# Attention plan: maxima placed by a count of VectorE's work against TensorE's

## The reference

```python
attn = jnp.einsum('bhqd,bhkd->bhqk', q, k) / np.sqrt(HD)
attn = jnp.where(mask[None, None], -jnp.inf, attn)
attn = jax.nn.softmax(attn, axis=-1)
out = jnp.einsum('bhqk,bhkd->bhqd', attn, v)
```

## Time and profile before

| | us |
|---|---|
| median of 3 runs | 1292.87 |
| lowest and highest | 1291.17, 1295.96 |
| the profiled execution | 1295.78 |
| its span, first to last instruction | 1294.5 |
| PE busy in it | 1202.9 |
| DVE busy | 897.0 |
| ACT busy | 661.0 |
| POOL busy | 602.1 |

### The profile page before, as it was taken

How to read it: one execution, slowest core, us unless ns; L and a number is a source line. 1 busy time by engine, 2 the same in 40 slices (tenths; PEclk the granted TensorE clock), 3 DMA queues, 4 the chain that set the end, 5 groups by cost and what they waited for, 6 DMA issues and landing times.

```text
span 1294.5 us, 22123 instructions
## 1 busy us (share of the span) xinstructions
PE 1202.9 (93%) x7422; PEld 781.6 (60%) x7429; DVE 897.0 (69%) x2100; ACT 661.0 (51%) x1313; POOL 602.1 (47%) x496
## 2 busy tenths in 40 slices
PE   4899999989998999999999999989999989999996
PEld 3578888758776554444545455545444447777774
DVE  7767777679996666575667677587754685666664
ACT  2545555525546554354456566356567733444442
POOL 5835445314200111001426556465682373888886
PEclk9899999999999999999989999999999999999999
DMA  9923333565620032023345845656743353666665
GB/s 345 354 90 109 105 114 107 163 181 104 109 48 32 4 68 34 1 96 50 86 124 139 164 99 111 183 131 157 138 99 66 109 210 74 104 103 101 101 103 73
DMA packets 68557, 148.52 MB, mean 115 GB/s; under 512 B 8832, under 2 KB 29312, under 8 KB 64448
## 3 DMA queue, kind: packets, MB, share of 16 engines
q0 software_dynamic: 35184, 93.34, 34.2%
q1 hardware_dynamic: 33264, 53.77, 12.1%
HBM read 81.28 MB, written 33.55 MB: 89 GB/s over the span
## 4 chain that ended last, share of the span: by engine, by line
PE 60%; DVE 17%; DMA 9%; issue 7%; POOL 4%; ACT 3%; SPq 0%; DVEq 0%; POOLq 0%; ACTq 0%
PE bank L1637 10%; PE bank L839 9%; PE bank L1649 9%; PE bank L997 8%; PE bank L862 5%; PE bank L1667 4%; PE bank L1704 3%; DMA out<-Y,DI 3%; DMA XG<-xn,TK 3%; POOL out L789 3%; DVE PM L1010 3%; DVE bank L1012 2%; PE bank L821 2%; PE bank L1398 2%; DMA CD<-P 1%
## 5 line engine op out<-in xcount | busy, mean ns | idle before, releaser
L1756 ACT ACTIVATE P<-bank 128x512 f32<-128x512 f32 (+3 forms) x640 | 303.8, 535 | 259.4 <-PE bank L1637 252.7
L1010 DVE TENSOR_REDUCE PM<-bank 128x1 f32<-128x512 f32 x384 | 252.8, 686 | 82.5 <-PE bank L997 81.9
L1637 PE MATMUL bank<-Qs,Ks 98*128 98x512 f32 (+3 forms) x640 | 241.1, 407 | 5.0 <-ACT P L1756 2.8
L997 PE MATMUL bank<-Ks,Qs 96*128 96x512 f32 (+3 forms) x640 | 234.6, 387 | 10.7 <-DVE PM L1012 5.4
L1637 PEld LDWEIGHTS bank<-Qs,Ks 98*128 98x128 f32 x640 | 116.9, 190 | 130.8 <-issue 59.5
L1795 POOL TENSOR_SCALAR_AFFINE_SELECT P<-P 128x512 f32<-128x512 f32 x64 | 42.9, 682 | 284.6 <-ACT P L1756 234.9
L1012 DVE CUSTOM_DVE_ANT_0 bank<-bank,KB 128x128 f32<-128x128 f32 (+3 forms) x256 | 124.8, 499 | 56.5 <-PE bank L997 55.9
L997 PEld LDWEIGHTS bank<-Ks,Qs 96*128 96x128 f32 x640 | 121.5, 191 | 57.6 <-DVE PM L1010 17.3
L1649 PE MATMUL bank<-P,V 128*32 128x512 f32 (+3 forms) x1280 | 150.9, 543 | 3.9 <-POOL P L1795 3.9
L789 POOL DMA_INDIRECT out<-Y,DI x78 | 127.1, 1629 | 40.7 <-issue 33.9
L1809 POOL TENSOR_TENSOR CH<-CH,P 128x512 f32<-128x512 f32 x108 | 139.3, 1438 | 14.0 <-ACT P L1756 13.3
(11 more groups left out here) (190 smaller groups left out, 1987.8 us busy)
## 6 DMA issues: line engine op xcount, KB each, us to landing
CD<-P POOLq DMA_DIRECT2D x17, 1024.0 KB, 7.3
xn<-XN SPq DMA_DIRECT2D x8, 1024.0 KB, 7.1
WR<-L_ffn_w POOLq DMA_DIRECT2D x16, 512.0 KB, 15.4
XO<-y POOLq DMA_DIRECT2D x8, 1024.0 KB, 9.8
WR<-L_ffn_w SPq DMA_DIRECT2D x16, 512.0 KB, 8.4
CD<-P SPq DMA_DIRECT2D x7, 1024.0 KB, 5.2
CD<-CH POOLq DMA_DIRECT2D x7, 1024.0 KB, 7.0
XA<-y POOLq DMA_DIRECT2D x24, 256.0 KB, 4.2
```

Source lines behind the costliest of these rows:

```text
L997: pe.matmul(bk(g, bank)[:, 0:n], g.Qs[b][0:96, G % 4 * 4 + h, c * P:c * P + P], g.Ks[0:96, G % 4, k * BQ:k * BQ + n], start=True, stop=Tru ...
L1010: dve.tensor_reduce(dst, bk(g, bank)[:, 0:n], AX.X, ALU.max).then_inc(s(f"free{bank}"), 1)
L1637: pe.matmul(bk(g, bank)[:, o:BQ], g.Ks[0:98, G % 4, k * P:k * P + P], g.Qs[G // 4][0:98, G % 4 * 4 + j, o:BQ], start=True, stop=True).then ...
L1756: act.activation(a.P4[buffer_of(n)][:, j, o:BQ], bk(g, score_bank(g, i))[:, o:BQ], ACT.Exp, scale=scale).then_inc(s("exp"), 1)
```

## The change

The widths are replaced by a count of work. A new class `Load` adds up, over the plan so far, units of PE's work (a full-width score or top is 1, a weigh 5 or 9, others from a table) and of DVE's work (a full-width top is 2.9, others from a table). Behind each score the count is brought up to date once, and then in up to two rounds a top is added unless DVE's count is above 0.81 of PE's. The start of the scores with five banks now looks for the last top or foundcopy and goes 2 steps behind it, where it looked for the last top and went 8 steps behind.

```diff
+DVE_SHARE = 0.81
+
+class Load:
+
+    PE = {"proj": 15, "tsum": 3, "even": 4, "found": 3, "turn": 2, "logits": 5, "best": 1}
+    DVE = {"proj": 3, "stats": 3, "solve": 6, "scale": 2.5, "tsum": 1, "even": 3, "solvemax": 3, "logits": 1.5, "best": 4.5}
+
+    def __init__(self):
+        self.pe = self.dve = 0.0
+
+    def add(self, plan, counted):
+        for step in plan[counted:]:
+            kind = step[0]
+            if kind in ("score", "weigh"):
+                G, k = TILES[step[1]]
+                wide = (BQ - first(G // 4, k)) / BQ
+                self.pe += wide if kind == "score" else wide * (8 if step[1] in SUMMED else 4) + 1
+            elif kind == "top":
+                wide = 1 if step[4] < step[1] // 4 else (step[3] + 1) / 4
+                self.pe += wide
+                self.dve += 0.6 + 2.3 * wide
+            else:
+                self.pe += self.PE.get(kind, 0)
+                self.dve += self.DVE.get(kind, 0)
+        return len(plan)
...
-    told, weight, given, extra, known, copying, free = 4, 0.0, 0.0, [], [], [], True
+    told, extra, known, copying, free, load, counted = 4, [], [], [], True, Load(), 0
...
             plan.append(("score", n, j))
-            weight += (BQ - first(b, k)) / BQ
-            while ahead and given < 1.1 * weight:
+            counted = load.add(plan, counted)
+            for _ in range(2):
+                if not ahead or load.dve > DVE_SHARE * load.pe:
+                    break
                 key = ahead.pop(0)
-                given += 1 if key[4] < key[1] // 4 else (key[3] + 1) / 4
                 plan.append(key)
...
-    last = max(at for at, step in enumerate(plan) if step[0] == "top")
-    g.wide = min(4 * step[1] + step[2] for step in plan[last + 8:] if step[0] == "score")
+    last = max(at for at, step in enumerate(plan) if step[0] in ("top", "foundcopy"))
+    g.wide = min(4 * step[1] + step[2] for step in plan[last + 2:] if step[0] == "score")
```

## The result

| | us |
|---|---|
| changed kernel, median of 4 runs | 1322.72 (1320.48 to 1326.5) |
| kernel before, same comparison | 1294.29 (1291.17 to 1295.96) |
| ratio, 95% interval | 1.0215 (1.0193 to 1.0237) |
| span of the profiled execution | 1322.2 |

The change makes the kernel 2.2% slower, 28 us. I had forecast slower, by 10 us, with a range up to 1318. The direction and the main term, waits for a bank behind bursts of tops, were right; what the change gives back was mis-sized, and score waits that I had put at nothing were not nothing.

A forecast was written before the change was run, and what follows sets the result against it. PE sets the pace, with DVE costing it some 22 us. Terms 18 + 3 + 1.5 - 3 - 3.5 - 4.5 - 1.5 = +10 us give 1305.8, on the median's scale 1303 us; range 1285 to 1318.

The forecast's parts named there:

- (1): Tops in bursts wait for their PSUM bank: 24.6 us after, less 6.6 now, +18 us.
- (2): Runs of six and eight tops are held by DVE's 0.60 us a top: +3 us.
- The 1.18 us: Full-width tops: a bank's next user starts 1.18 us, or five units, after the top that held it.
- Rival A, relief wins: PE's waits at tile ends are the dear ones, nearly all 22 us come back: 1283 us, chance 0.15.
- (3): Tops behind found wait longer for the bank that ScalarE's copy at L1068 frees: +1.5 us.
- (4): PE's waits for DVE backlog go: found -3 us, tsum and L1667 -3.5, tops -4.5.
- The 4.5 us for backlog: Tops' waits behind projections, statistics and best shrink as the count slows tops there: -4.5 of 5.9 us.
- (5): At 599 to 603 us found and best no longer share a tile: -1.5 us, with its clock.
- (6): The end: last top and five-bank scores start later, no DMA or Pool step moves but maxima copies: 0.
- My signs: L997 weight loads wait 40 us or more in over 100 places, L1059 under 4 us; wrong if PEclk drops.
- rival C: PE's short gaps make its clock drop, ten more drops at 1.6 us: 1319 us, chance 0.1.

The follow-up runs named there:

- e1: Kernel before with its old budget, but two tops whenever one is due: 1304.8 us, 1.0078.
- e2: Changed kernel, same table and 0.81, but counted after each top and the coming weigh counted in quarters: 1304.62 us, 1.0068.
- e11: Kernel before with tops in pairs and DVE reading half of each top's columns: 1275.37 us, 0.9845.
- e3: Changed kernel with DVE reading only half of each top's columns (half maxima): 1296.6 us, 1.0016.
- e6: Kernel before with only the change's last two lines, the later start of five-bank scores: 1296.5 us, 1.0002.
- e9: Changed kernel with half maxima, variance by tensor_reduce and a copy in place of ScalarE's square root in the statistics: 1286.6 us, 0.9937.
- e10: Kernel before with half maxima, variance by tensor_reduce and a copy in place of ScalarE's square root in the statistics: 1267.44 us, 0.9797.
- e5: Changed kernel with the statistics' variance made by tensor_reduce instead of L299's tensor_scalar, 1e-5 left out: 1321.01 us, 1.0195.

## Why the prediction was wrong, point by point

*Bank waits and long runs, (1) and (2): right.* Forecast +18 and +3, measured +21.7 where a top follows a top. The subtraction in (1) was not clean: it took 6.6 us, reckoned without the correction for earlier waits, from 24.6, reckoned with it. Like for like it is 24.6 - 4.2 = +20.4. The 1.18 us recurs (479.33 to 480.51), and e1, e2 and e11 speak for the bank: pairs cost 10 us, undoing the bursts gives 19 back, and with a faster DVE pairs cost nothing that could be measured. For the changed kernel itself it is shown less well: with half maxima top behind top lost 18 us less, but the gap to the kernel before closed by 5 us only, or by some 9 at equal clock. Rival A, relief wins, falls with the result.

*The bank of "found", (3): right.* PE itself waits 3.4 us in 8 places for L1068's copy, where it waited 2.0 in 5; I had said +1.5.

*Relief, (4): mis-sized.* I gave back 11 us; about 5 came. Top before weigh or tsum went from 4.7 to 1.1 us as forecast. But weigh before found gave 0.9 us, not 3. My reading, which no run separates, is that a burst makes DVE as late at the tile's end as evenly spaced tops do, and that only fewer tops in that very tile help. The 4.5 us for backlog cannot be found in any row, and PE now waits a little before tsum, projections and turns (score before tsum 0 to 0.8 us, top before projection 0.6 to 1.1, within a projection 0.1 to 0.8).

*One stall, (5): failed.* I forecast -1.5 us. Scores 160 to 191 lost 4.6 us before and 5.0 after. The stall at 603 us went, others came. The half-clock time beside it did shrink (4.7 to 2.8 us), and grew again in other profiles (e3: 11.2).

*The steps that failed* are therefore the relief in (4) and (5), put at 12.5 us where about 5 came, and one that I left out: I put the scores' own waits at nothing. I priced tops as filler that may be anywhere. When ScalarE falls behind (square root with two table loads, copies of outputs, sums and maxima), a score waits for the exponential three scores back, and what PE can do meanwhile is the tops between the scores. In the changed plan the five worst of these places have none. The row score behind score grew by 9.5 us, but the stretches compared above by 4.0 us, plus up to 1.9 for the eight tops done elsewhere. Of the 4.0, 3.1 are not the missing filler: in (6) I wrote that nothing but the copies of maxima moves among the scores, and what moved with the tops around them was when DVE's small operations fall against POOL's additions, which took 3.10 us for L299. That this one met them is chance; the forecast had no term for it.

*My signs.* The weight loads of tops waited 43.2 us for DVE (38.4 and 4.8), over the 40 that I had named, but in 90 places, not over 100. L1059 did not fall under 4 us. The clock showed no more low digits.

*The sum by measured terms:* 21.7 + 9.5, less about 5 of relief and changes in the other rows, is about the 25.8 us of the table; my own was 21 + 1.5 - 12.5. The remaining 3 to 4 us of the 28 lie outside the attention in the profiles (first score 2.0 us later, and 1.6 us more behind the last) and I have no cause for them; the plan doesn't touch those stages. (6) held: e6 shows nothing from the later five banks.

*What stays open.* Of the 18 us between e9 and e10, 8 are top behind top and 4 score behind score by the same reckoning, and 6 score behind top; I did not separate the last. One kind of wait that I had not looked for is in it: ScalarE's exponential held by a DMA that still reads P (CD<-P). In the waits view ScalarE waits for it 2.9 us (once) before and 7.2 us (3 times) in the changed kernel, where score 271 lost PE 1.41 us at 728.67 behind a transfer of 13.46 us; in e10 it is 6.7 us (3) and in e9 11.1 (4). How much of this comes from the order of the tops was not tested. *The clock, rival C,* isn't the cause of the result, but the share of half-clock time differs from run to run of the same kernel (e3's runs had a granted clock of 0.972 to 0.988, and took 1305.9 to 1290.4 us), so single differences of 2 to 4 us may be that.

## What to carry to other kernels

A budget that evens out two engines' work over a stretch says nothing about what a ring of three banks can hold: check each burst against the bank's recycling time (here 0.44 + 0.69 + 0.05 us) before the average. A debt that is reckoned after a long step gets paid in a burst; reckon it before, in parts, and bring the count up to date after every item. And look at where the *other* engine stalls before taking filler away there: here it cost a top's time in a few places, and a shift of small operations against a third engine's cost more.

## What the runs showed of the hardware

A DVE tensor_scalar on 128x4 elements of SBUF lasted 3.10 us beside POOL's tensor_tensor (1.86 and 3.61 us in two other kernels, 0.17 when POOL was idle), ending within 0.05 us of POOL's row. POOL's additions start 1.22 to 1.25 us apart (880.52, 881.77, 883.01, 884.23), so the instruction was held over the start of two more of them, to the end of the series. A tensor_reduce of the same elements took 0.16 us in e5, amid such a series of additions. A DVE maximum over 256 PSUM columns took 0.425 us against 0.686 over 512.
